# The row-maxima shift of an attention kernel, as four 32-row products for two key tiles at once

## The chip, the cores and the metric

The kernel runs on one core of one Trainium2 chip. The metric is the device time of one execution in microseconds (us); the kernel before takes 3069.19 us, the median of three runs (3068.3 to 3076.0). TensorE (PE) multiplies, VectorE (DVE), ScalarE (ACT) and GpSimd (POOL) work beside it, each with its own queue of instructions in order; they meet through semaphores only.

## The reference

Two layers on `x` of shape (2, 256, 64, 64), all in float32:

```
xn  = group_norm(x, 32 groups)
qkv = qkv_weight @ xn + qkv_bias            # 4 heads of 64 channels, 4096 positions
a   = softmax over the second position of (q^T k) / 8
out = a applied to v, then proj_weight @ out + proj_bias
x1  = x + out
h   = conv3x3(relu(batch_norm(x1)), mean|w0| * sign(w0))
y   = conv3x3(relu(batch_norm(h)),  mean|w1| * sign(w1)) + x1
```

Softmax is exact up to a common factor in a row, so any number can be taken from a row's scores before the exponential. The kernel takes the row's maximum.

## The kernel before, in words

Attention is done for one batch entry and one pair of heads at a time: four **pairs**, one after the other. The two heads of a pair lie on the partitions 0 to 63 and 64 to 127 (`own[0]`, `own[1]`), since a head has 64 channels. Each pair first projects q, k and v (`project`), and splits q and k in two halves of 16 bits each (`q_hi + q_lo`, `k_hi + k_lo`).

Then come 8 **query blocks** of 512 queries (`query_block`, L691), so 32 in all, numbered by `it`. A block walks over 32 **key tiles** (`kt`) of 128 keys in 16 **groups** of two. The scores of one key tile are a 128 x 512 matrix for each head, and fill two PSUM banks; `ps_s` has two slots of two banks, one for the even and one for the odd tile of a group. For each tile (`scores`, L676) TensorE issues three pairs of products (L683: `k_hi q_hi`, `k_lo q_hi`, `k_hi q_lo`), each pair one product for each head, with 64 rows of the array each, side by side. A fourth pair (L688) takes the row maxima off: the left factor `shift` is a matrix with the constant 32768 in the first four rows of each head's half and zero elsewhere, and the right factor `m_rows` has in its first four rows the negated maxima of the 512 queries divided by 32768, each query's in one of the four rows. With the 60 zero rows that is a product of 64 rows too.

ScalarE waits for the tile's count on `s_ready` and takes the exponential of both heads in one instruction of 128 x 1024 (L544) into `prob`, which has six buffers. TensorE multiplies the probabilities by v two tiles later (`values`, L672, float32, both heads side by side as 128 rows by 64 columns). The sums of the probabilities are made by GpSimd (L492; all tiles, or one head alone for 16 of the 32), with the other head of these 16 done by VectorE (L841, L844). GpSimd adds VectorE's half at the end of a block (L495), for which it waits until ScalarE has copied it (`copy_half`, L558), and this ScalarE does behind the exponential of `kt == 1` of the next block. TensorE then adds over partitions (`column_sums`, L663), in group 2 of the next block, or, for the last block of a pair, right behind it.

The maxima of the *next* block are found beside this one: TensorE makes the scores roughly from `k_hi` and `q_hi` alone (`next_maxima`, L648, 64-row pairs into the two banks of `ps_max`), VectorE reduces them (L788), and only then may the next go into the same banks (`mx_used`). A block has 32 of these units: two in a group ("early" and "late"), three in groups 6 and 11 (one more in the middle, "mid"), none in group 15 (`units_of`, L72). The last block of a pair has no next one, and so none. In groups 4 and 5 VectorE also divides the output of the block before (L811, L820). In group 14 it finishes the maxima (L792, L795), in group 15 TensorE turns them into rows (`max_rows`, L655), and VectorE writes `m_rows` from them (`write_max_rows`, L797 to L804, an instruction for each head). TensorE waits for these (`m_rows_done`, L686) ahead of the shift of the block's first tile. For a pair's first block, all this is done before the block starts.

The order of TensorE's work in a group is written out by hand: scores of the even tile, mid, scores of the odd tile, early, (row products in group 15), values of the two tiles before, (column sums in group 2), late. After the two pairs of a batch entry come the output projection and the residual sum, and after all of attention the two convolutions, whose products (L1111) run in 16 steps of 96. The change leaves these alone.

Of the kernel before, what the change touches and what calls it, by code (L numbers as in the profile page):

```python
# [36 lines left out]
QT = TB // P  # L37
# [9 lines left out]
SHIFT = 32768.0  # L47
# [24 lines left out]
def units_of(group):  # L72

    if group >= ROWS_AT:
        return [], [], []
    first = 2 * group + sum(m < group for m in MID_AT)
    if group in MID_AT:
        return [first], [first + 1], [first + 2]
    return [], [first], [first + 1]
# [91 lines left out]
def prologue(nc, x, qkv_t, proj_t, w0_t, par_d, const_d, g):  # L171
    par, const, ones = g.par, g.const, g.ones
    with ExitStack() as ctx:
        def sem(name):
            return ctx.enter_context(nc.semaphore(name))
# [28 lines left out]
        pool_set = sem("pool_set")  # L204
# [3 lines left out]
        @block.sync  # L208
        def _(sp):
            for i in range(B * CB):  # L210
                sp.dma_start(xf[:, i, :], x[i // CB, i % CB]).then_inc(xf_in[i], 16)

            for s in range(2):
                sp.dma_start(g.xn[:, s], x[0, :, :, s * TB:(s + 1) * TB].rearrange("c p n -> p c n")).then_inc(
                    g.xn_in[s], 16)
            sp.dma_start(g.wst[:].rearrange("p c j o -> p (c j o)"), qkv_t[0]).then_inc(g.w_staged, 16)
            sp.dma_start(g.wf[:], w0_t[0]).then_inc(g.wf_in, 16)
# [17 lines left out]
        @block.gpsimd  # L235
        def _(pool):
            nc.gpsimd.memset(ones[:], 1.0).then_inc(pool_set, 1)
            pool.wait_ge(pool_set, 1)

            nc.gpsimd.memset(g.m_rows[:], 0.0).then_inc(pool_set, 1)  # L240
            nc.gpsimd.memset(g.shift[:], 0.0).then_inc(pool_set, 1)
            pool.wait_ge(pool_set, 3)
            for h in range(2):
                s0 = g.own[h].start
                nc.gpsimd.memset(g.shift[s0:s0 + QT, :], SHIFT).then_inc(pool_set, 1)
            pool.wait_ge(pool_set, 5)
            pool.wait_ge(loc_ready, 1)
            nc.gpsimd.partition_all_reduce(g.bound[:], loc[:], P, RMAX).then_inc(bound_ready, 1)

# [95 lines left out]
def attention(nc, x, qkv_t, w0_t, x1_d, g):  # L345
    xt, y32, wst, x1t = g.xt, g.y32, g.wst, g.y_tile
    own, xn, shift, m_rows = g.own, g.xn, g.shift, g.m_rows
    ident = g.const[:, IDENT:IDENT + P]
    mask = g.const[0:QT, MASK:MASK + TB].rearrange("p (a n) -> p a n", a=QT)
    with ExitStack() as ctx:  # L350
        def sem(name):
            return ctx.enter_context(nc.semaphore(name))
# [25 lines left out]
        s_ready = sem("s_ready")  # L378
# [12 lines left out]
        m_rows_done = sem("m_rows_done")  # L391
# [6 lines left out]
        def cols(i, n=TB):  # L398
            return bass.ds(i * n, n)
# [194 lines left out]
        def _(pe):  # L594
            mm = nc.tensor.matmul
# [46 lines left out]
            def next_maxima(it, qb, units):  # L642

                for u in units:
                    t, kb = u // NB, u % NB
                    pe.wait_ge(mx_used, 1 + it * UNITS + u)
                    for h in range(2):
                        last = mm(g.ps_max[:, h], q_hi[own[h], qb * TB + t * P:qb * TB + (t + 1) * P],  # L648
                                  k_hi[own[h], kb * TB:(kb + 1) * TB], start=True, stop=True)
                    last.then_inc(mx_ready, 1)  # L650

            def max_rows(it):
                pe.wait_ge(m_neg_ready, it + 1)
                for h in range(2):
                    last = mm(g.ps_max[0:QT, 1, h * P:(h + 1) * P], m_neg[:, h * QT:(h + 1) * QT], ident,  # L655
                              start=True, stop=True)
                last.then_inc(m_rows_ready, 1)

            def column_sums(it):

                pe.wait_ge(tot_ready, it + 1)
                for h in range(2):
                    last = mm(g.ps_misc[own[h], :], g.ones[:, 0:HD], acc_pool[:, it % 2, h * TB:(h + 1) * TB],  # L663
                              start=True, stop=True)
                last.then_inc(sum_ready, 1)

            def values(n):

                pe.wait_ge(exp_done, n + 1)
                kt = n % KT  # L670
                for h in range(2):
                    last = mm(g.ps_o[own[h], :], vals[:, kt, own[h]], prob[:, n % PBUF, h * TB:(h + 1) * TB],  # L672
                              start=(kt == 0), stop=(kt == KT - 1))
                last.then_inc(g.pv_done, 1)

            def scores(it, qb, kt, first):  # L676

                if kt >= 2 or not first:
                    pe.wait_ge(exp_done, it * KT + (kt - 1))
                keys = slice(kt * P, (kt + 1) * P)  # L680
                for k, q in ((k_hi, q_hi), (k_lo, q_hi), (k_hi, q_lo)):
                    for h in range(2):
                        mm(g.ps_s[:, kt % 2, h], k[own[h], keys], q[own[h], cols(qb)], start=(k is k_hi and q is q_hi),  # L683
                           stop=False)
                if kt == 0:
                    pe.wait_ge(m_rows_done, (it + 1) * 2)  # L686
                for h in range(2):
                    last = mm(g.ps_s[:, kt % 2, h], shift[own[h]], m_rows[own[h], qb % 2], start=False, stop=True)  # L688
                last.then_inc(s_ready, 1)

            def query_block(it, qb):  # L691

                first, last = qb == 0, qb == NB - 1
                for group in range(GROUPS_A):
                    kt = 2 * group
                    mid, early, late = ([], [], []) if last else units_of(group)
                    scores(it, qb, kt, first)
                    next_maxima(it + 1, qb + 1, mid)
                    scores(it, qb, kt + 1, first)
                    next_maxima(it + 1, qb + 1, early)  # L700
                    if group == ROWS_AT and not last:
                        max_rows(it + 1)
                    if group == 1 and not first:
                        pe.wait_ge(o_copied, it + 1)
                    if group or not first:
                        for old in (kt - 2, kt - 1):
                            values(it * KT + old)
                    if group == SUMS_AT and not first:
                        column_sums(it - 1)
                    next_maxima(it + 1, qb + 1, late)  # L710
                if last:
                    for old in (KT - 2, KT - 1):
                        values(it * KT + old)
# [12 lines left out]
            for b in range(0, B):  # L726
                for hp in range(0, 2):
                    pair = b * 2 + hp
                    it0 = pair * NB
                    for s in range(2):  # L730
                        project(b, hp, 0, s, False)
                    for n2 in range(1, NB // 2):
                        for s in range(2):
                            project(b, hp, n2, s, True)
                    for s in range(2):
                        first_maxima(it0, NB // 2 - 1, s, range(QT))

                    pe.wait_ge(klo_done, 2 + it0 + NB)
                    pe.wait_ge(qlo_done, 2 + it0 + NB)
                    pe.wait_ge(v_copied, 2 + it0 + NB)  # L740
                    max_rows(it0)
                    for qb in range(NB):
                        query_block(it0 + qb, qb)
                    column_sums(it0 + (NB - 1))

                for n2 in range(0, NB // 2 - 1):
                    for s in range(2):
                        output_projection(b, n2, s, 1)
                output_projection(b, NB // 2 - 1, 0, 1)
                output_projection(b, NB // 2 - 1, 1, 0)  # L750

        @block.vector
        def _(dve):
# [43 lines left out]
            def write_max_rows(it, slot):  # L797

                dve.wait_ge(m_rows_ready, it + 1)
                for h in range(2):  # L800
                    s0 = own[h].start
                    v.tensor_tensor(m_rows[s0:s0 + QT, slot].rearrange("p (a n) -> p a n", a=QT),  # L802
                                    g.ps_max[0:QT, 1, h * P:(h + 1) * P].unsqueeze(1).to_broadcast([QT, QT, P]),
                                    mask, ALU.mult).then_inc(m_rows_done, 1)  # L804
# [473 lines left out]
```

## Time and profile before

| | us |
|---|---|
| median of three runs | 3069.19 |
| profiled execution, its own time | 3075.72 |
| its span, from the first to the last instruction | 3073.9 |
| mean granted TensorE clock | 0.972 of 2.4 GHz |

```
engine                       busy us   share of span
PE (matmul)                   2829.9   92%
DVE                           2145.2   70%
POOL                          2025.5   66%
ACT                           1390.7   45%
```

TensorE is busy in 92% of the span, but products overlap in the records, so that this is no measure of its load: the start times of products tell it. A product of 512 columns is recorded with 0.38 us, and the next pair starts about 0.22 us after it. The two products of a pair start within 0.01 us of each other, and the views merge them ("x2"). Attention's blocks run from 118 us to about 2650 us of the span, with projections between the pairs. A release that names L688 is the shift, with which a score tile becomes ready for ScalarE.

### The profile page before, as it was taken

The page shows a single profiled execution, that of the slowest core. Times are in us where ns is not written, and L with a number is a line of the kernel's source. Part 1 is how long each engine was busy: PE and PEld are TensorE (multiplying, and loading weights), DVE is VectorE, ACT ScalarE, POOL GpSimd, SP SyncE. Part 2 cuts the span into 40 slices and gives each one's busy share as a digit, 9 for nine tenths or more (in the row PEclk, how much of TensorE's full clock was granted, in tenths as well). Part 3 has the DMA queues.
Part 4 walks back from the last instruction along what each step waited for, and adds up shares of the span by engine and source line. Part 5 has one row for each costly group of instructions (what it writes and reads, how often), then busy time and mean ns, then how long its engine had stood idle before and what let it go on. Part 6 is the DMA issues. An engine that isn't in the chain of part 4 may idle for free. (4 is left out here: it accounts for less than half of the span.)

```text
span 3073.9 us, 43595 instructions
## 1 busy us (share of the span) xinstructions
PE 2829.9 (92%) x17060; PEld 1013.5 (33%) x17060; DVE 2145.2 (70%) x2528; ACT 1390.7 (45%) x1461; POOL 2025.5 (66%) x1208
## 2 busy tenths in 40 slices
PE   5799999997999999987999999987999999979898
PEld 3233333323333333333333333342333333334343
DVE  5677777736777777546777777456777776488785
ACT  3354444452545444532544454543454445344342
POOL 2588778783888888843888888855878888520022
PEclk9899999998999999998999999998999999989999
DMA  5000000001000000041000000010000000232032
GB/s 203 33 1 1 1 1 1 1 1 60 1 1 1 1 1 1 1 132 54 1 1 1 1 1 1 1 42 1 1 1 1 1 1 1 71 116 88 0 109 82
DMA packets 26819, 78.27 MB, mean 25 GB/s; under 512 B 1920, under 2 KB 2176, under 8 KB 25600
## 3 DMA queue, kind: packets, MB, share of 16 engines
q1 hardware_dynamic: 25792, 74.19, 6.9%
q8 instruction: 125, 2.05, 0.3%
q10 hardware_dynamic: 832, 1.45, 0.1%
q14 instruction: 70, 0.57, 0.1%
HBM read 58.86 MB, written 16.78 MB: 25 GB/s over the span
## 5 line engine op out<-in xcount | busy, mean ns | idle before, releaser
L492 POOL TENSOR_TENSOR acc_pool<-acc_pool,prob 128x512 f32<-128x512 f32 (+1 forms) x992 | 1779.6, 1794 | 376.9 <-ACT prob L544 269.9
L544 ACT ACTIVATE prob<-ps,exp_scale 128x1024 f32<-128x1024 f32 x1024 | 1091.9, 1111 | 1191.0 <-PE ps L688 1188.5
L788 DVE TENSOR_REDUCE m_part<-ps 128x2 f32<-128x1024 f32 x896 | 1095.2, 1222 | 477.6 <-PE ps L648 453.6
L672 PE MATMUL ps<-prob,vals 128*64 128x512 f32 x4096 | 999.8, 609 | 0.0
L648 PE MATMUL ps<-k_hi,q_hi 64*128 64x512 f16 x1792 | 347.5, 384 | 79.8 <-DVE m_part L788 79.8
L672 PEld LDWEIGHTS ps<-prob,vals 128*64 128x64 f32 x4096 | 250.3, 137 | 498.5 <-issue 367.4
L844 DVE TENSOR_TENSOR ps<-ps,prob 128x512 f32<-128x512 f32 x480 | 331.5, 691 | 91.2 <-ACT prob L544 91.2
L683 PE MATMUL ps<-q_hi,k_hi 64*128 64x512 f16 x2048 | 391.8, 379 | 0.0
L683 PE MATMUL ps<-q_hi,k_lo 64*128 64x512 f16 x2048 | 391.0, 378 | 0.0
L683 PE MATMUL ps<-q_lo,k_hi 64*128 64x512 f16 x2048 | 390.8, 378 | 0.0
L688 PE MATMUL ps<-m_rows,shift 64*128 64x512 f16 x2048 | 390.4, 378 | 0.4
L648 PEld LDWEIGHTS ps<-k_hi,q_hi 64*128 64x128 f16 x1792 | 86.6, 93 | 522.6 <-DVE m_part L788 451.3
L773 DVE TENSOR_REDUCE m_part<-ps 128x2 f32<-128x1024 f32 x128 | 156.9, 1226 | 104.7 <-PE ps L638 104.7
L1111 PE MATMUL ps<-parts,signs 128*128 128x512 f16 x768 | 181.3, 385 | 21.9 <-DVE parts L1170 19.9
L811 DVE RECIPROCAL ps<-ps 128x128 f32<-128x128 f32 x128 | 122.7, 959 | 99.3 <-PE ps L663 99.3
L1111 PE MATMUL ps<-parts,wmid 128*128 128x512 f16 x768 | 179.0, 383 | 0.0
L683 PEld LDWEIGHTS ps<-q_hi,k_hi 64*128 64x128 f16 x2048 | 100.4, 95 | 126.9 <-ACT prob L544 45.5
L688 PEld LDWEIGHTS ps<-m_rows,shift 64*128 64x128 f16 x2048 | 100.0, 94 | 125.8 <-DVE m_rows L802 4.0
L683 PEld LDWEIGHTS ps<-q_lo,k_hi 64*128 64x128 f16 x2048 | 100.2, 95 | 122.9 <-issue 2.7
L609 PE MATMUL ps<-xn,wst 128*128 128x512 f32 x256 | 129.7, 636 | 8.1 <-ACT xn L582 5.2
L683 PEld LDWEIGHTS ps<-q_hi,k_lo 64*128 64x128 f16 x2048 | 100.1, 94 | 111.3 <-issue 1.6
L525 ACT ACTIVATE y<-ps,pair_bias,fscale 128x512 f32<-128x512 f32 x64 | 49.7, 777 | 175.2 <-PE ps L609 127.1
(115 smaller groups left out, 1587.8 us busy)
## 6 DMA issues: line engine op xcount, KB each, us to landing
xt<-in_x SPq DMA_DIRECT2D x40, 512.0 KB, 4.0
xf<-in_x SPq DMA_DIRECT2D x4, 2048.0 KB, 17.0
x_scratch<-y_tile SPq DMA_DIRECT2D x16, 512.0 KB, 5.0
wf<-in_w_t SPq DMA_DIRECT2D x4, 1152.0 KB, 9.9
rows<-x_scratch SPq DMA_DIRECT2D x8, 576.0 KB, 5.1
rows<-x_scratch SPq DMA_DIRECT2D x8, 544.0 KB, 4.6
xn<-in_x SPq DMA_DIRECT2D x8, 512.0 KB, 5.7
xt<-x_scratch SPq DMA_DIRECT2D x4, 1024.0 KB, 5.1
```

Source lines behind the costliest of these rows:

```text
L492: nc.gpsimd.tensor_tensor(acc[:, part], acc[:, part], tile[:, part], ALU.add).then_inc(pool_add, 1)
L544: nc.scalar.activation(prob[:, n % PBUF], g.ps_s[:, kt % 2].rearrange("p h n -> p (h n)"), ACT.Exp, scale=g.exp_scale[:]).then_inc(exp_don ...
L609: ins = mm(g.ps_s[:, s, j], wst[:, c, j, :], xn[:, s, c, :], start=(c == 0), stop=(c == CB - 1))
L648: last = mm(g.ps_max[:, h], q_hi[own[h], qb * TB + t * P:qb * TB + (t + 1) * P], k_hi[own[h], kb * TB:(kb + 1) * TB], start=True, stop=True)
L672: last = mm(g.ps_o[own[h], :], vals[:, kt, own[h]], prob[:, n % PBUF, h * TB:(h + 1) * TB], start=(kt == 0), stop=(kt == KT - 1))
L683: mm(g.ps_s[:, kt % 2, h], k[own[h], keys], q[own[h], cols(qb)], start=(k is k_hi and q is q_hi), stop=False)
L688: last = mm(g.ps_s[:, kt % 2, h], shift[own[h]], m_rows[own[h], qb % 2], start=False, stop=True)
L773: v.tensor_reduce(m_part[:, :, t * NB + (n2 * 2 + s)], g.ps_max, AX.X, ALU.max).then_inc(mx_used, 1)
L788: v.tensor_reduce(m_part[:, :, u], g.ps_max, AX.X, ALU.max).then_inc(mx_used, 1)
L811: v.reciprocal(g.ps_misc[:, c], g.ps_misc[:, c]).then_inc(rec_ready, 1)
L844: v.tensor_tensor(acc_dve, acc_dve, tile, ALU.add).then_inc(dve_add, 1)
L1111: last = nc.tensor.matmul(g.ps[:, 4 * m + pos, :], weights(l, c, pos, dx)[:, m * P:(m + 1) * P], parts[:, s, c, h, pos, :, dx:dx + W], sta ...
```

## The change

The shift leaves `scores` and becomes a step of its own, `shifts`, once a group, behind the scores of both tiles and ahead of the early maxima. It consists of four products of 32 rows: row quarter r holds the constants and maxima rows for head r % 2, and the product goes to tile r // 2 of the group. So quarters 0 and 1 serve the even tile, 2 and 3 the odd one, in four different PSUM banks. `s_ready` rises by two when the last is done, so that both tiles come free for ScalarE at once. The quarters 1 and 3 need rows of their own: `write_max_rows` has four instructions for two, and the setting of `shift` in the prologue four for two.

```diff
@@ prologue, GpSimd
-            for h in range(2):
-                s0 = g.own[h].start
-                nc.gpsimd.memset(g.shift[s0:s0 + QT, :], SHIFT).then_inc(pool_set, 1)
-            pool.wait_ge(pool_set, 5)
+            for r in range(4):
+                nc.gpsimd.memset(g.shift[32 * r:32 * r + QT, :], SHIFT).then_inc(pool_set, 1)
+            pool.wait_ge(pool_set, 7)
@@ attention, TensorE
+            def shifts(it, qb, kt):
+
                 if kt == 0:
-                    pe.wait_ge(m_rows_done, (it + 1) * 2)
-                for h in range(2):
-                    last = mm(g.ps_s[:, kt % 2, h], shift[own[h]], m_rows[own[h], qb % 2], start=False, stop=True)
-                last.then_inc(s_ready, 1)
+                    pe.wait_ge(m_rows_done, (it + 1) * 4)
+                for r in range(4):
+                    quarter = slice(32 * r, 32 * r + 32)
+                    last = mm(g.ps_s[:, r // 2, r % 2], shift[quarter], m_rows[quarter, qb % 2], start=False, stop=True)
+                last.then_inc(s_ready, 2)
@@ query_block, TensorE
                     scores(it, qb, kt, first)
                     next_maxima(it + 1, qb + 1, mid)
                     scores(it, qb, kt + 1, first)
+                    shifts(it, qb, kt)
                     next_maxima(it + 1, qb + 1, early)
@@ write_max_rows, VectorE
-                for h in range(2):
-                    s0 = own[h].start
+                for r in range(4):
+                    s0, h = 32 * r, r % 2
```

## Rows read from the trace of the kernel before

**Rows 1.** Page: the shift's products (count; busy us, mean ns; idle before).
```profile
L688 PE MATMUL ps<-m_rows,shift 64*128 64x512 f16 x2048 | 390.4, 378 | 0.4
```
**Rows 2.** Timeline of PE, an ordinary group (start us, us, what, count).
```profile
1000.05 0.38 PE L683 MATMUL ps<-q_hi,k_hi 64*128 64x512 f16 x2
...
1001.56 0.38 PE L688 MATMUL ps<-m_rows,shift 64*128 64x512 f16 x2
1001.77 0.38 PE L648 MATMUL ps<-k_hi,q_hi 64*128 64x512 f16 x2
1002.08 1.94 PE L672 MATMUL ps<-prob,vals 128*64 128x512 f32 x8
1003.95 0.39 PE L648 MATMUL ps<-k_hi,q_hi 64*128 64x512 f16 x2
1004.18 0.38 PE L683 MATMUL ps<-q_hi,k_hi 64*128 64x512 f16 x2
```
**Rows 3.** Stretch of group 7: us, busy of PE, PEld, DVE, ACT, POOL.
```profile
1012.80:1016.90 4.10, 4.10 (x30) 1.38 (x28) 3.63 (x5) 2.12 (x2) 3.08 (x3) 1.00 0.00 0
```
**Rows 4.** Timeline of PE, groups 6 and 11: maxima that wait for VectorE.
```profile
1006.68 0.38 PE L688 MATMUL ps<-m_rows,shift 64*128 64x512 f16 x2
1008.33 0.59 PE L648 MATMUL ps<-k_hi,q_hi 64*128 64x512 f16 x2 [1.27 <-DVE m_part L788]
...
1030.41 0.39 PE L648 MATMUL ps<-k_hi,q_hi 64*128 64x512 f16 x2 [0.46 <-DVE m_part L788]
...
1032.13 0.39 PE L648 MATMUL ps<-k_hi,q_hi 64*128 64x512 f16 x2 [0.47 <-DVE m_part L788]
```
**Rows 5.** A pair's last block: waits, GpSimd's groups 622.8 to 685.3, timeline.
```profile
PE ps L663 <- POOL acc_pool L495: 22.8, 4, 5.7
...
L492 POOL TENSOR_TENSOR acc_pool<-acc_pool,prob 128x512 f32<-128x512 f32 (+1 forms) x31 | 55.6, 1794 | 4.4
...
621.62 1.27 POOL L495 TENSOR_TENSOR acc_pool<-acc_pool,half_sum 128x512 f32<-128x512 f32 x1 [1.04 <-ACT half_sum L558]
...
618.88 2.12 ACT L544 ACTIVATE prob<-ps,exp_scale 128x1024 f32<-128x1024 f32 x2 [2.23 <-PE ps L688]
```
**Rows 6.** Changes of tile shape: weight loads (group 5), group 15, line L655.
```profile
1002.56 0.14 PEld L672 LDWEIGHTS ps<-prob,vals 128*64 128x64 f32 x2 [0.29 <-ACT prob L544]
1002.99 0.14 PEld L672 LDWEIGHTS ps<-prob,vals 128*64 128x64 f32 x2 [0.28 <-issue]
...
1048.45 0.38 PE L688 MATMUL ps<-m_rows,shift 64*128 64x512 f16 x2
1048.89 0.60 PE L655 MATMUL ps<-const,m_neg 128*4 128x128 f32 x4
1049.42 1.94 PE L672 MATMUL ps<-prob,vals 128*64 128x512 f32 x8
...
L655 PE MATMUL ps<-const,m_neg x128: 272/273/421, 115.9 to 2590.8; 128*4 128x128 f32 x128
```
**Rows 7.** Timelines of DVE and PE: rows of maxima written, next block's scores.
```profile
1049.53 1.39 DVE L802 TENSOR_TENSOR m_rows<-ps,const 4x512 f16<-4x512 f32 x2
...
1051.29 0.39 PE L683 MATMUL ps<-q_hi,k_hi 64*128 64x512 f16 x2
```
**Rows 8.** Timeline at the start of a pair's first block.
```profile
765.36 1.39 DVE L802 TENSOR_TENSOR m_rows<-ps,const 4x512 f16<-4x512 f32 x2 [1.20 <-PE ps L655]
...
768.91 0.64 PE L648 MATMUL ps<-k_hi,q_hi 64*128 64x512 f16 x2
...
770.87 0.39 PE L648 MATMUL ps<-k_hi,q_hi 64*128 64x512 f16 x2 [1.32 <-DVE m_part L788]
```
**Rows 9.** Stretches at half clock (as rows 3, then PEclk); values in one.
```profile
359.60:363.00 3.40, 3.15 (x8) 0.87 (x10) 2.02 (x3) 0.14 (x1) 3.11 (x3) 0.54 0.00 0
...
2407.60:2411.00 3.40, 3.31 (x10) 0.86 (x10) 1.86 (x3) 0.00 (x0) 3.11 (x3) 0.54 0.01 2
...
1008.85 3.38 PE L672 MATMUL ps<-prob,vals 128*64 128x512 f32 x8
```

## The prediction

> **What bounds the kernel now.** I read the page first for what the change touches: 2048 shift products of 0.38 us each, with no idle time ahead of them, so TensorE comes to them with everything ready [rows 1]. Next the order in time on TensorE for one ordinary group. The reader is to look at start times, not at durations. From 1000.05 to 1001.77 eight pairs start, one every 0.215 us: that is a pair's price, and of the recorded 0.38 us the rest lies under the next pair. Two of the eight are shifts. Then come the values and the late maxima, and the same point of the next group is at 1004.18: 4.13 us a group, without a gap [rows 2]. In such a group TensorE sets the pace: the other engines are busy for less than its 4.10 us, VectorE 3.63, GpSimd 3.08, ScalarE 2.12 [rows 3].
>
> Not every group is like that. Where three maxima stand in a group, TensorE waits for VectorE: in group 6 for 1.27 us, since VectorE comes late out of the divisions of groups 4 and 5, and in group 11 twice for some 0.47, because a maximum can't follow the last sooner than 1.72 us (1030.41 to 1032.13), the time of product, reduction and release [rows 4]. In group 15 the products on the maxima's rows start 0.44 us after the last shift, where 0.31 is what a change of work costs elsewhere [rows 2, 6]: that is a wait for VectorE too. So of 16 groups five (4, 5, 6, 11 and 15) have VectorE's pace, and 11 have TensorE's. There are 4 x 7 = 28 blocks that look ahead, so 28 x 11 = 308 groups in which a change of TensorE's work counts in full. The last block of a pair is another case: GpSimd adds 31 tiles there with 4.4 us of idle time in all, and TensorE then waits for it at the column sums, four times, 22.8 us in sum [rows 5]. That block ends with GpSimd, and faster products there buy nothing.
>
> **The shift's products.** Removed are two pairs, 2 x 0.215 = 0.43 us a group. Added are four products of 32 rows. If they run side by side as pairs do now, they take one slot of 0.215, and about 0.01 for two more starts. On this alone the group would be 0.205 us shorter. But now a third shape of tile stands in the middle of the 64-row products, and what it costs to change the shape can be read. From the last 64-row pair to the values (128 rows, 64 columns) it is 0.31 us, where a pair takes 0.215: 0.095 more [rows 2]. The other way, the values' four pairs at 0.43 each [rows 6] make 1.72, and the next 64-row pair starts 1.87 after the first of them [rows 2]: 0.15 more, of which 0.095 would be the way out and 0.055 the slower loading at the way in. For the 16-bit pair that follows, the way in costs 0.01 (0.39 us for 0.38, [rows 2]). A third case has 128 rows on both sides and differs in columns alone: four products on the maxima's rows at (0.60 - 0.27) / 3 = 0.11 make 0.44, and the values start after 0.53: 0.09 more [rows 6]. So every change of shape in this trace costs 0.09 on the way out and 0.01 to 0.055 on the way in. None shows 32 rows beside 64. I take for it what all the others have, with the way in of 16-bit data, 0.10 for one change and 0.20 for two. New price: 0.215 + 0.01 + 0.20 = 0.425, for 0.43 before. Over 308 groups that is -1.5 us, and as the rows have only hundredths, **0 +- 3 us**. The bounds: with no change to pay, -0.205 a group, -63 us; with two at 0.15, 0.525 for 0.43, +29 us.
>
> The Trainium skill (TensorEngine Tiling (Array Packing), Key Properties) says that going to another tiling mode, not just to another tile, drains TensorE. The 0.09 us above [rows 2, 6] is what such a drain costs here, and the page would have it for 32 rows against 64 as well; by it the sum is the 0 just taken. The same skill (TensorE: Matmul & The Clock Gate, Part 3, measured speedup) has four row tiles of 32 with 512 columns at 3.07 times the speed of one after another. An estimate from it is 0.86 / 3.07 = 0.28 us for the four and not 0.225, +0.055 a group, +17 us; no run here shows that yet.
>
> **The even tile comes later.** Its shift used to start behind its own scores; now it waits for the odd tile's scores, some 0.65 + 0.10 us. Both exponentials follow at once, 2.12 us in all, from 0.42 us after the shift started [rows 5], counted from the shift of the same group, so they end 1.5 and 2.6 us after the new shift. Who waits for them? The next even scores start 0.31 + 0.31 + 1.87 + 0.23 = 2.7 us after the shift (maxima, values, maxima), the next odd ones at 3.4, and values a whole group later: cover of 1.2 and 0.8 us. In the last blocks, without maxima, these are 0.31 + 1.87 = 2.2 and 2.8 us against 1.5 and 2.6: still cover, 0.2 at the least. **0 us**; were it gone there, GpSimd still ends last. VectorE adds a tile's half only behind a maximum that starts later. 0.
>
> There is one place without cover. At a pair's last block GpSimd is the bound, and before it starts its 32 tiles it waits 1.04 us for ScalarE's copy of the half sum, which stands behind the second exponential of the block [rows 5]. Now: exponentials from 618.88, done at 621.00. After: the scores of both tiles are six pairs, which end where the old second shift's start less 0.215 was, so the new shift starts about 0.12 us before the old second one did, 0.74 after the old first one, and the exponentials and the copy are 0.75 us later. GpSimd's chain moves with them: 4 x 0.75 = **+3 us**. For the 28 other blocks this copy is late too, but the column sums wait for it only in group 2, over 4 us later: 0.
>
> **The rows of maxima.** VectorE writes four times, not twice; two took 1.39 us, so four take 2.8, and from 1049.53 they end at 1052.33. TensorE needs them ahead of the new shift: the next block's scores start at 1051.29, six pairs make 1.30 and the change of shape 0.09, so 1052.68 [rows 7]. Cover 0.3 us, thin; each 0.1 us that is lacking would cost 28 x 0.1 = 3 us. VectorE itself has no maxima in group 15. At a pair's first block the writing is open to view: from 765.36 four end at 768.16, so a shift at 768.2, and at the half clock of that stretch early maxima 0.43 + 0.2 later, 768.85, for 768.91 now; what comes next waits at 770.87 for the reduction of just these [rows 8]. **0**. Two more settings in the prologue are small work of an engine that has nothing else to do there. 0.
>
> **The clock.** In group 6 TensorE's idle time is sometimes followed by 3.4 us at half clock (0.54 as the mean of the stretch, so 1.2 GHz); there are six such stretches, one in the group 6 of six of the 28 blocks. The values then take 3.38 us for 1.94 and the maxima ahead 0.59 for 0.39: 1.6 us each [rows 2, 4, 9]. In groups 5 and 6 the wait on VectorE stays and TensorE has less to stream around it, so I count one more, **+2 us**.
>
> **Sum.** 0 + 3 + 0 + 2 = +5 us. The profiled execution took 3075.72 (its span 3073.9 and 1.8 around it), 6.5 above the median of 3069.19, and would take 3080.7; the median becomes **3074 us**.
>
> **Rivals.**
> A. *32 and 64 rows change without a drain*, both being cuts of the same rows. Then 308 x 0.205 = 63 us go: 3074 - 63 = **3011**. The other engines would allow it: early maxima come 1.95 us behind late ones now and may come 1.72 behind, so 0.23 is to be had there [rows 2, 4]. Against it: each of the kinds of change that the trace has costs the same, even where the rows stay 128.
> B. *The four don't run side by side*, but two and two, for a port or a bank that four share. Then the change saves nothing and pays the two changes of shape: +0.215 x 308 = 66, **3140**. It decides from the point where the third product starts a slot behind the first. For it: nothing in the trace has more than two tiles at once. Against: the two products of a pair start within 0.01 us and write two banks; here four write four. This is the rival on the other side.
> C. *The clock falls in every group 6*: 22 more times 1.6 is 35, less the 2 counted, **3107**. For it: the idle time is in each block. Against: it takes it in six of 28 now, and the change adds no wait there.
> D. *A change of shape is dearer than 0.10*, with four weights to load at once, 0.15 as before the values: +29, **3103**.
>
> **How the numbers follow.** My forecast 0.53, with a range of its own from 3066 to 3083 (the +-3, one to three stretches of clock, cover that fails a little); A 0.18; D 0.11; C 0.07; B 0.07; 0.04 for others. From no change a measurement of this kernel can tell about 0.3%, 9 us. Within it: most of the forecast, 0.52. Faster: A and a rest, 0.20. Slower: D, C, B and a rest, 0.28. The range goes from A to C, 3006 to 3110; left out are B, the lower edge of A and others, some 0.15.
>
> **What would show it.** In the order in time on TensorE: the four shift products start within 0.02 us; the first of them 0.31 after the last scores, the early maxima 0.31 to 0.33 after it; an ordinary group still 4.13 us from point to point. If the distances are 0.215, A is right, and the group is 3.9; if third and fourth start 0.2 later, B. The exponentials come in twos right behind each other, and GpSimd's add of the half in a pair's last block is 0.75 us later against the block's first scores. Six to eight stretches at half clock in group 6. The forecast is wrong if an ordinary group differs from 4.13 by more than 0.03 us.

## The result and the profile after

The changed kernel takes 3083.0 us (13 runs, 3072.5 to 3089.0) for 3068.7 (13 runs of the kernel before beside them): 1.0045 times the time, interval 1.0032 to 1.0058. A later batch gave 3082.1 (5 runs) and a ratio of 1.0037 (1.0023 to 1.0051). The prediction was 3074 with a range of 3006 to 3110. So the time lies in the range and near the forecast, but 9 us above it, and beyond the 0.3% that I had called no change. One execution of the kernel before, in the batch of the first experiments, took 4911.8 us at a granted clock of 0.607 and is left out of every median and mean. The profiled execution took 3082.3 us, with a span of 3080.5 and a mean granted clock of 0.969.

The page has the shift's products at half their busy time (203 us for 390), as four of 32 rows now stand side by side:

```profile
L691 PE MATMUL ps<-m_rows,shift 32*128 32x512 f16 x2048 | 203.2, 387 | 1.3 <-DVE m_rows L806 1.3
```

The time did not follow. The timeline of TensorE for an ordinary group, as [rows 2] has it for before (start us, us, what, count):

```profile
1044.76 0.39 PE L647 MATMUL ps<-k_hi,q_hi 64*128 64x512 f16 x2
1044.98 0.38 PE L682 MATMUL ps<-q_hi,k_hi 64*128 64x512 f16 x2
...
1046.06 0.38 PE L682 MATMUL ps<-q_lo,k_hi 64*128 64x512 f16 x2
1046.37 0.40 PE L691 MATMUL ps<-m_rows,shift 32*128 32x512 f16 x4
1046.70 0.39 PE L647 MATMUL ps<-k_hi,q_hi 64*128 64x512 f16 x2
1047.02 1.94 PE L671 MATMUL ps<-prob,vals 128*64 128x512 f32 x8
1048.89 0.39 PE L647 MATMUL ps<-k_hi,q_hi 64*128 64x512 f16 x2
1049.12 0.38 PE L682 MATMUL ps<-q_hi,k_hi 64*128 64x512 f16 x2
```

The reader is to see three distances. From the last scores to the shift it is 0.31 us, from the shift to the maxima 0.33, where pairs of one shape follow each other in 0.215: two changes of tile shape at 0.1 each, one on each side of the shift. And the record of the four lasts 0.40 us for 0.38, so they do run side by side. The group is 4.14 us from 1044.98 to 1049.12, for 4.13 before. The slot that was saved has been paid out again.

At a pair's last block, GpSimd and ScalarE, for [rows 5]:

```profile
621.68 2.12 ACT L543 ACTIVATE prob<-ps,exp_scale 128x1024 f32<-128x1024 f32 x2 [2.24 <-PE ps L691]
...
624.43 1.27 POOL L494 TENSOR_TENSOR acc_pool<-acc_pool,half_sum 128x512 f32<-128x512 f32 x1 [1.05 <-ACT half_sum L557]
...
688.17 1.97 PE L662 MATMUL ps<-acc_pool,ones 128*64 128x512 f32 x4 [7.43 <-POOL acc_pool L494]
```

The block's first scores start at 619.83, so the exponentials are 1.85 us behind them (before 618.88 - 617.80 = 1.08). From the add of the half sum to the column sums nothing has moved: 63.74 us for 63.71. TensorE now waits there for 7.43 us, 5.7 before: it is ready about 0.9 us earlier, and GpSimd comes 0.8 later, both against the block's first scores.

The four writes of maxima rows, for [rows 7]; the second row is the shift behind them:

```profile
618.07 2.82 DVE L806 TENSOR_TENSOR m_rows<-ps,const 4x512 f16<-4x512 f32 x4
...
621.23 0.40 PE L691 MATMUL ps<-m_rows,shift 32*128 32x512 f16 x4
```

They end at 620.89; the shift starts 0.31 us after the last scores (620.92), as everywhere, so it did not wait.

Last, group 6 and the clock, for [rows 4, 9]. In the stretches the third figure from the end is the granted clock; there are seven like these in the 28 blocks that look ahead, the first and the last shown.

```profile
1008.11 0.39 PE L647 MATMUL ps<-k_hi,q_hi 64*128 64x512 f16 x2 [0.82 <-DVE m_part L792]
...
1009.08 0.39 PE L691 MATMUL ps<-m_rows,shift 32*128 32x512 f16 x4
1010.62 0.61 PE L647 MATMUL ps<-k_hi,q_hi 64*128 64x512 f16 x2 [1.16 <-DVE m_part L792]
1011.16 3.23 PE L671 MATMUL ps<-prob,vals 128*64 128x512 f32 x8
...
361.60:365.00 3.40, 3.19 (x10) 0.86 (x10) 1.97 (x3) 1.22 (x2) 3.26 (x2) 0.54 0.00 0
...
2413.00:2416.40 3.40, 3.11 (x8) 0.87 (x10) 2.06 (x3) 1.31 (x2) 3.26 (x2) 0.54 0.00 0
```

A block without such a stretch takes 71.1 us from first exponential to first exponential in both kernels, and one with it 72.7 to 72.8.

### The profile page after: what moved, and what is told of

The parts are those of the page before. It is cut to its first block and busy times, and to the rows that moved or that the text cites. A ratio compares the mean times of both kernels' runs of the same rounds, so it can differ in the third digit from the quotient of the medians.

```text
span 3080.5 us, 43661 instructions
## 1 busy us (share of the span) xinstructions
PE 2821.7 (92%) x17060; PEld 966.5 (31%) x17060; DVE 2188.8 (71%) x2592; ACT 1381.8 (45%) x1461; POOL 2025.5 (66%) x1210
## 5 line engine op out<-in xcount | busy, mean ns | idle before, releaser
L691 PE MATMUL ps<-m_rows,shift 32*128 32x512 f16 x2048 | 203.2, 387 | 1.3 <-DVE m_rows L806 1.3
L1065 ACT ACTIVATE parts<-comb 128x512 f16<-128x512 f32 x128 | 77.4, 632 | 105.8 <-DVE comb L1195 105.8
```

The costliest lines, as they stand in the source:

```text
L691: last = mm(g.ps_s[:, r // 2, r % 2], shift[quarter], m_rows[quarter, qb % 2], start=False, stop=True)
```

## The experiments

Each run comes with its granted clock, and since the clock is either full or half, twice (1 - clock) times the span is its time at half clock. The table has, beside the median time, the means over the runs of each kernel. The last column takes off half of the time at half clock, as if TensorE had set the pace throughout it (a pair of products then takes 0.43 us for 0.215). That is the most that can be lost. Among the runs of one kernel the span grows by only about a third of it (a straight line through the runs has a slope of 0.37 for before, 0.33 for changed).

| kernel | runs | median us | clock | at half clock, us | span less half of it |
|---|---|---|---|---|---|
| before | 20 | 3070.1 | 0.9741 | 159 | 2988 |
| changed | 13 | 3083.0 | 0.9690 | 191 | 2985 |
| before, again | 11 | 3071.7 | 0.9736 | 162 | 2989 |
| changed, again | 5 | 3082.1 | 0.9702 | 184 | 2987 |
| order alone | 11 | 3064.8 | 0.9765 | 144 | 2992 |
| order, one pair | 4 | 2996.2 | 0.9718 | 169 | 2911 |
| before, divisions moved | 5 | 3052.1 | 0.9764 | 144 | 2979 |
| changed, divisions moved | 5 | 3056.9 | 0.9752 | 152 | 2979 |
| 32 rows at each tile | 4 | 3234.8 | 0.9765 | 152 | 3155 |
| behind the maxima | 5 | 3120.0 | 0.9734 | 166 | 3035 |
| order alone, copy ahead | 6 | 3062.2 | 0.9767 | 143 | 2989 |
| changed, copy ahead | 12 | 3073.8 | 0.9713 | 176 | 2984 |
| the fastest | 5 | 3044.8 | 0.9754 | 150 | 2969 |

**Before and changed, again.** The same kernels; only clocks and stretches are wanted.

> The kernel before, run as an experiment of its own, so that each of its runs comes with its granted clock. The changed kernel's 13 runs have mean clocks from 0.966 to 0.972, and their times lie between 3089 and 3073 in the same order: half of the time at half clock is lost. Theory 1 (the surplus of the change over my sum, some 9 us, is time at half clock): runs of before lie at a higher clock than those of after, 0.970 to 0.975, and time less (1 - clock) x span is the same for both kernels within 3 us. Theory 2 (the surplus is a wait in every run, in the first blocks and at the ends of the pairs): the clocks are alike, about 0.969, and that corrected time is 10 us or more lower for before. Time against before: the same within 0.2% in both.

> The changed kernel once more, beside the same runs of before as the next three. In the first batch before had a mean granted clock of 0.974 in 31 runs, and the order alone (64-row products behind both tiles' scores) 0.9765 and 3065 us. Time less (1 - clock) x span: changed 2985, before 2988, order alone 2992. If the whole surplus of the change is time at half clock: again 3081 to 3084, clock 0.969, in its profile six to nine stretches of 3.4 us behind the wait of group 6, where the order alone had none in 28 blocks and before four to six.

Before against before has a ratio of 1.0005 (0.9996 to 1.0014). Its clock is 0.0046 above that of the changed kernel, and less half of the time at half clock the two are 3 us apart, the changed one lower; with a third in place of the half the changed one is some 2 us higher. Theory 1 holds either way: the surplus is mostly time at half clock. Its profile has four stretches at half clock in group 6 (289.1, 504.1, 1756.8 and 2401.9), that of [rows 9] six. The changed kernel has six in its second profile, seven in its first.

**The order alone**, against the kernel before:

```diff
-                for h in range(2):
-                    last = mm(g.ps_s[:, kt % 2, h], shift[own[h]], m_rows[own[h], qb % 2], start=False, stop=True)
-                last.then_inc(s_ready, 1)
+            def shifts(it, qb, kt):
...
+                for t in range(2):
+                    for h in range(2):
+                        last = mm(g.ps_s[:, t, h], shift[own[h]], m_rows[own[h], qb % 2], start=False, stop=True)
+                last.then_inc(s_ready, 2)
@@ query_block
                     scores(it, qb, kt + 1, first)
+                    shifts(it, qb, kt)
```

> Only the order of the change: the four shift products keep 64 rows (two pairs), but stand behind the scores of both tiles, and both tiles are released at once. Two writes of maxima rows, no third shape of tile. If the change's price for shape just cancels the slot that it saves (my sum), the ordinary group is 4.13 us here as in both kernels, and GpSimd's chain in a pair's last block is late by 0.85 us (the even tile waits for 0.86 us of products), 3 to 4 us in all: 3069 + 4 = 3073. If the surplus of the change comes with the order (exponentials in twos, more time at half clock around group 6), this kernel has it too: 3080 to 3085. If it comes with 32-row products (less load on TensorE, so a lower clock, or the four writes of rows), this one stays at 3073.

3064.8 us, 0.9985 of before (0.9976 to 0.9994): faster, which none of my cases had. The group is what it was:

```profile
1007.20 0.38 PE L683 MATMUL ps<-q_hi,k_hi 64*128 64x512 f16 x2
...
1008.28 0.38 PE L683 MATMUL ps<-q_lo,k_hi 64*128 64x512 f16 x2
1008.49 0.59 PE L691 MATMUL ps<-m_rows,shift 64*128 64x512 f16 x4
1008.93 0.38 PE L648 MATMUL ps<-k_hi,q_hi 64*128 64x512 f16 x2
1009.24 1.94 PE L672 MATMUL ps<-prob,vals 128*64 128x512 f32 x8
...
1011.33 0.38 PE L683 MATMUL ps<-q_hi,k_hi 64*128 64x512 f16 x2
```

4.13 us, with 0.21 ahead of the shift and 0.44 (two slots) for it. And in 28 blocks there is no stretch at half clock in group 6, though TensorE waits there nearly as long as in the changed kernel (0.82 and 1.05 us, for 0.82 and 1.16):

```profile
1002.26 0.39 PE L648 MATMUL ps<-k_hi,q_hi 64*128 64x512 f16 x2 [0.82 <-DVE m_part L792]
...
1003.14 0.59 PE L691 MATMUL ps<-m_rows,shift 64*128 64x512 f16 x4
1004.78 0.39 PE L648 MATMUL ps<-k_hi,q_hi 64*128 64x512 f16 x2 [1.05 <-DVE m_part L792]
1005.10 1.94 PE L672 MATMUL ps<-prob,vals 128*64 128x512 f32 x8
...
1001.40:1004.80 3.40, 1.53 (x16) 0.53 (x14) 3.29 (x5) 1.03 (x2) 3.11 (x3) 1.00 0.00 0
```

So the surplus comes with the 32-row products (or the four writes, which this kernel doesn't have either), not with the order. The order alone has the late exponentials as well: in its last blocks the column sums start 68.46 us behind the first scores, for 67.54 before and 68.34 in the changed kernel.

**32 rows at each tile**, the price of a change of shape by itself, in the kernel before:

```diff
-                    last = mm(g.ps_s[:, kt % 2, h], shift[own[h]], m_rows[own[h], qb % 2], start=False, stop=True)
+                    rows = slice(own[h].start, own[h].start + 32)
+                    last = mm(g.ps_s[:, kt % 2, h], shift[rows], m_rows[rows, qb % 2], start=False, stop=True)
```

> The kernel before with one thing changed: the two shift products of a tile have 32 rows (0 to 31 and 64 to 95) in place of 64, where they stood. No slot is saved, and each tile pays two changes of shape, so two groups of them a group. By my price of 0.10 for one change, an ordinary group is 4.13 + 0.40 = 4.53 us, and 308 groups make +123 us; group 11 and group 6 absorb theirs: 3069 + 120 = 3190 (3175 to 3205). If 32 rows beside 64 cost nothing (rival A), 3069. If a change costs 0.05, 3130.

3234.8 us, 1.0537 times before (1.0520 to 1.0553).

```profile
1052.12 0.38 PE L683 MATMUL ps<-q_hi,k_hi 64*128 64x512 f16 x2
...
1052.55 0.38 PE L683 MATMUL ps<-q_lo,k_hi 64*128 64x512 f16 x2
1052.87 0.39 PE L689 MATMUL ps<-m_rows,shift 32*128 32x512 f16 x2
1053.18 0.39 PE L683 MATMUL ps<-q_hi,k_hi 64*128 64x512 f16 x2
```

0.32 and 0.31 us where 0.215 stood: rival A is out, and one change costs 0.10 each way. The group is 4.55 us. The total is 45 us above what I expected: a block takes 76.6 us for 71.1, so 28 x 5.5 = 154 and not 123. That is 13 groups' worth of 0.42, where I had counted 11: groups 4 and 5 count in full too (4.55 us each, as the others), and group 6, where VectorE's lateness covers the products, becomes only 0.14 us shorter by it (6.43 for 6.57). The rest lies mainly in the pairs' last blocks (69.7 us for 67.5 from the first scores to the column sums). The clock did not fall here, with 32-row products and twice as many changes of shape: 0.9765, and one stretch at half clock in group 6. So it isn't 32 rows as such that lower it.

**Behind the maxima.** One change of shape fewer, from 32 rows straight to the values:

```diff
                     scores(it, qb, kt + 1, first)
-                    shifts(it, qb, kt)
+                    if group == 0:
+                        pe.wait_ge(m_rows_done, (it + 1) * 4)
                     next_maxima(it + 1, qb + 1, early)
+                    shifts(it, qb, kt)
```

> The changed kernel with the shifts behind the early maxima in place of ahead of them (the wait for the rows of maxima stays ahead of the maxima of group 0). TensorE then goes 64 rows, 32 rows, 128 rows for the values: one change of shape fewer in a group. By my price the ordinary group is 4.03 us, 308 x 0.10 = 31 us less than the changed kernel: 3083 - 31 = 3052, 0.5% below the kernel before. Rival: VectorE or the exponentials, which come 0.3 us later still, take up the 0.10, and the group stays at 4.13: 3083.

3120.0 us, 1.0161 times before (1.0147 to 1.0175): 37 us more than the changed kernel, where the rival said as much as it.

```profile
1025.09 0.39 PE L647 MATMUL ps<-k_hi,q_hi 64*128 64x512 f16 x2
...
1026.40 0.38 PE L682 MATMUL ps<-q_lo,k_hi 64*128 64x512 f16 x2
1026.81 0.39 PE L647 MATMUL ps<-k_hi,q_hi 64*128 64x512 f16 x2
1027.13 0.39 PE L689 MATMUL ps<-m_rows,shift 32*128 32x512 f16 x4
1027.45 1.94 PE L671 MATMUL ps<-prob,vals 128*64 128x512 f32 x8
1029.32 0.39 PE L647 MATMUL ps<-k_hi,q_hi 64*128 64x512 f16 x2
```

The changes are saved as planned, and the early maxima still wait: from the late ones there are only six pairs, 1.52 us, and they can follow in 1.72 at the least [rows 4]. So 1.72 + 0.32 + 0.32 + 1.87 = 4.23 us a group. The shift had stood between two maxima and covered VectorE's time. I had the 1.72 in the prediction and did not apply it here.

**One pair.** The order alone with the odd tile's shift left out:

```diff
-                           stop=False)
+                           stop=kt % 2 == 1 and q is q_lo)
...
-                for t in range(2):
-                    for h in range(2):
-                        last = mm(g.ps_s[:, t, h], shift[own[h]], m_rows[own[h], qb % 2], start=False, stop=True)
+                for h in range(2):
+                    last = mm(g.ps_s[:, 0, h], shift[own[h]], m_rows[own[h], qb % 2], start=False, stop=True)
```

> The order alone (64-row products once a group), with the odd tile's shift left out, so that its exponentials are of scores that nothing was taken from: TensorE's work a group is one pair of 64 rows for the shift and no third shape of tile. This is what the change would be if its two changes of shape cost nothing: an ordinary group 4.13 - 0.215 = 3.91 us. Maxima then follow each other in 1.73 us where 1.72 is the least, so VectorE just allows it. 11 groups of 28 blocks: 3065 - 66 = 2999 (2995 to 3010). If VectorE or GpSimd holds the group above 3.91, the change had no more than that to gain even with free changes of shape.

2996.2 us, 0.9761 of before (0.9747 to 0.9775), and 69 less than the order alone.

```profile
965.60 0.38 PE L683 MATMUL ps<-q_lo,k_hi 64*128 64x512 f16 x2
965.82 0.38 PE L690 MATMUL ps<-m_rows,shift 64*128 64x512 f16 x2
966.03 0.38 PE L648 MATMUL ps<-k_hi,q_hi 64*128 64x512 f16 x2
...
969.95 0.38 PE L648 MATMUL ps<-k_hi,q_hi 64*128 64x512 f16 x2
```

3.92 us from maxima to maxima: no other engine holds the group. So a slot saved would have been worth all of its 0.215, and the two changes of shape took just this. It also bears on the clock: two stretches at half clock came back in group 6, and 169 us in all for the 144 of the order alone, with 64-row products throughout and two writes. The two stretches are 7 of the 25 us. Some 14 stand at the pairs' ends, where TensorE waits for GpSimd ahead of the column sums: 8.2 us here, and the half clock that sets in during the wait lasts 10.2 us in all four pairs; in the order alone the wait is 6.6 and the half clock 6.8. The same 10 us around a wait, this kernel first (the granted clock is again the third figure from the end):

```profile
661.20:671.20 10.00, 5.59 (x9) 1.92 (x10) 3.39 (x6) 0.19 (x1) 4.13 (x3) 0.50 0.00 1
...
680.90:691.10 10.20, 8.68 (x28) 4.30 (x29) 4.75 (x8) 2.81 (x4) 2.54 (x3) 0.68 0.00 1
```

What this kernel shares with the changed one is that TensorE streams one slot less than in the order alone. It is also ready sooner wherever another engine sets the pace: in group 6 it waits 1.03 and 1.27 us, for 0.82 and 1.05 in the order alone, so that less work and a longer wait come together here.

**The divisions moved**, in the kernel before and in the changed one:

```diff
-DIVIDE_AT = {(4, 0): 0, (4, 1): 1, (5, 0): 2, (5, 1): 3}
+DIVIDE_AT = {(3, 0): 0, (4, 0): 1, (4, 1): 2, (5, 0): 3}
```

> The kernel before with VectorE's four divisions at (3,0), (4,0), (4,1), (5,0) in place of (4,0), (4,1), (5,0), (5,1), so that VectorE is not late at the three maxima of group 6. Group 6 should then look like group 11, 5.62 for 6.57 us: 28 x 0.95 = 27 us less, and no stretch at half clock in group 6 (4 to 6 now, 1.6 us each, 8 us): 3069 - 27 - 8 = 3034. If TensorE's wait in group 6 has another source than the divisions: 3069.

> The changed kernel with the same move of the divisions. Theory 1 (the surplus is half clock behind group 6's wait, plus 3 us at GpSimd's chain): without that wait this kernel is only 3 to 6 us above the kernel before with the same move, 3038 to 3040. Theory 2 (a surplus in every block or at the pairs' borders, with no tie to group 6): it stays 12 to 14 us above it, 3047. If 32-row products lower the clock anywhere TensorE waits, group 11 now shows stretches at half clock.

3052.1 us (0.9939, 0.9925 to 0.9952) and 3056.9 us (0.9949, 0.9936 to 0.9963). Of the 27 us that I expected for the shorter wait there were 11: a block is 70.7 us for 71.1 and group 6 still 6.15 where I had 5.62, since VectorE is still late at the first of the three maxima. But neither kernel has a stretch at half clock in group 6 any more, nor one in group 11, and the distance between the two fell from 11 to 14 us to 4.8. Theory 1 said 3 to 6. So 6 to 9 us of the surplus, more than half, seem tied to group 6; the runs of the two reach from 3051.4 to 3055.3 and from 3051.7 to 3059.9, so that this is good to some 4 us only.

**The copy ahead.** In a pair's last block, on the order alone and on the changed kernel:

```diff
+                if last:
+                    copy_half(it - 1)
                 for kt in range(KT):
...
                     if kt == 1 and not first:
-                        copy_half(it - 1)
+                        if not last:
+                            copy_half(it - 1)
                         copy_output(it - 1)
```

> The order alone (64-row products once a group), and in a pair's last block ScalarE copies VectorE's half sum ahead of the block's first exponential in place of behind the second. GpSimd's chain there then starts as soon as its last tile of the block before is added: about 1.0 us earlier than in the order alone, four times, 4 us: 3065 - 4 = 3061. If something else ends these blocks (the column sums or the first exponential), 3065. Theory on the change: of its surplus 3 us come from this copy, which this run measures by itself.

> The changed kernel with the half sum copied ahead of the first exponential in a pair's last block. If the late copy costs the change what I said, GpSimd's chain starts 1.0 us earlier at four places: 3082 - 4 = 3078, with 1.0 us less from the block's first exponential to the column sums (66.49 in the changed kernel). The four writes of rows delay the half sum itself, so it may be 0.5 us and 3080.

3062.2 us (0.9970, 0.9958 to 0.9982), 2.6 less than the order alone; and 3073.8 us for the changed kernel (1.0010, 0.9999 to 1.0020), some 8 less. GpSimd, with the copy ahead of the changed kernel's exponentials:

```profile
616.35 4.87 POOL L491 TENSOR_TENSOR acc_pool<-acc_pool,prob 128x1024 f32<-128x1024 f32 x2 [1.45 <-ACT prob L545]
621.30 1.27 POOL L494 TENSOR_TENSOR acc_pool<-acc_pool,half_sum 128x512 f32<-128x512 f32 x1
```

There is no wait for ScalarE left. From the block's first exponential to the column sums it is 65.29 us for 66.49. But that exponential itself now comes 0.34 us later behind the block's first scores, as the copy stands ahead of it; from these scores to the column sums it is 67.47 us for 68.34, so 0.87 are gained, 3.5 in four pairs. Of the 8 us that the medians show this leaves 4.7; having 8 us less at half clock (176 for 184) would give some 3 of them, and the rest I can't assign.

**The fastest.** Order alone, copy ahead, divisions at (3,0), (3,1), (4,0), (4,1):

> What the runs point to as the fastest: 64-row products once a group, the early copy, and the divisions at (3,0), (3,1), (4,0), (4,1), two half groups ahead of before. With the divisions at (3,0) to (5,0) a block was 70.7 us for 71.1, and group 5 still 5.73 where an undisturbed one is 5.20; without that 0.53 a block is 70.2: 28 x 0.9 = 25 us less than order and copy (3062), 3037, and no stretch at half clock in group 6. If the divisions only move the delay to groups 3 and 4, where there are two maxima and no third, TensorE waits there instead, and it is 3050.

3044.8 us, 0.9922 of before (0.9909 to 0.9935), the fastest complete kernel here; with 70.4 us a block, about halfway between my two cases. It has 64-row products only.

## Why the prediction was right, and where it was not

*Shift products: 0 +- 3 us.* Right, with its working. Four side by side cost one slot and two changes of shape cost 0.10 each (0.31 and 0.33 us around the shift); the group is 4.14 us for 4.13, a block 71.1 for 71.1. The two bounds were tested: without changes of shape 69 us are to be had (I had 63), and with two more pairs of changes a group grows by 0.42. That a change costs the same between 32 and 64 rows was the guess on which all depended, and the chance of 0.18 for rival A was fair for a shape that the trace did not have. The drain of the Trainium skill (TensorEngine Tiling (Array Packing), Key Properties) is thus shown here with its price. The estimate from its other page (the Trainium skill, TensorE: Matmul & The Clock Gate, Part 3, measured speedup) of 0.28 us for the four is not borne out: the group would be 4.18 us, and of the 0.33 from the shift to the maxima 0.10 are the change of shape, which leaves 0.23.

*How many groups count: 308.* Too few, since groups 4 and 5 have TensorE's pace and not VectorE's. The block without a slot is 68.5 us for 71.1, 12 groups' worth (13 groups are shorter by a slot, and group 6 is longer by one, 6.78 us for 6.57), and the one with dearer groups 13's. As the price of a group was next to nothing, this did no harm to the sum.

*The even tile later: 0, and +3 at the last blocks.* Right in its reading, too much for the total. No scores and no values wait for an exponential in an ordinary group; in the last blocks scores wait for one eight times, 1.8 us in all, at no cost, as GpSimd ends last. GpSimd's chain is 0.8 us late against the first scores in each of four blocks, 3.2 us.

*The rows of maxima: 0.* Right in the other blocks (no wait at 621.23, cover 0.3). In a pair's first block it is 73.8 us for 73.4 from `m_neg` (the negated maxima, made ahead of the block) to the second block's first exponential. That isn't a term beside the last one. An exponential stands 0.77 us further behind its scores in every block, so by its scores the second block comes 0.3 us earlier. Over a whole pair, from `m_neg` to the column sums of the last block, both are in: with the divisions moved, where no block has a stretch at half clock, it is 564.4 and 564.6 us in two pairs of the changed kernel and 563.9 to 564.1 in the four of before. (The other two pairs of the changed kernel take 566.0 and 567.5, with 9.6 and 14.6 us at half clock for about 8.) So all that is late comes to 0.5 us a pair, **2 us** in all; 3.2 and four times 0.45 would count the later exponential twice.

*The clock: +2 us.* This term failed by its size, and it is what puts the result outside 0.3%. I counted stretches in the one profile I had, six, and added one. The changed kernel's profiles have seven and six, so that this looks right; but the count in before's execution was high for it: again it had four, and its mean clock over 20 runs is 0.974, for 0.969. In time at half clock the kernels differ by 191 - 159 = 32 us, and by 22 in the later batch. With the third that the runs of one kernel lose of it, an estimate, that is 11 and 7 us. With the wait of group 6 shortened, 6 to 9 us of the surplus go. The profiles show less than that in group 6 itself: seven and six for six and four, at 1.65 us each (72.77 us for a block of 71.12). Rival C had the mechanism, in a size (every block) that did not come. The sign was right, and "less to stream around it" fits: the order alone (a slot more, no stretch), one pair (a slot less, two stretches, 64 rows) and the changed kernel (a slot less and two changes of shape, six and seven) go up in this row. What is not shown is that the load alone decides. One pair's waits in group 6 are the longest of the three, with fewer stretches than the changed kernel, so the length of the wait alone doesn't either. Two executions of one kernel have stretches in different blocks and in different number, and in these kernels the blocks also lie at other times; no run holds one fixed and moves the other.

What I had not thought of at all are the pairs' ends. TensorE waits 7.2 to 7.5 us there for GpSimd, 5.7 before, and the half clock around this wait lasts 10.2 us in two of the four pairs in either profile of the changed kernel; in the two profiles of the kernel before it lasts 6.8 in all eight. Ten us around such a wait, changed and before:

```profile
2662.40:2672.60 10.20, 5.75 (x9) 2.08 (x10) 3.56 (x7) 2.20 (x2) 4.17 (x3) 0.50 0.00 0
...
2657.50:2667.70 10.20, 7.26 (x15) 2.84 (x16) 4.79 (x9) 2.14 (x2) 2.81 (x2) 0.69 0.00 1
```

Added up: 2 us of delays, 0 for the groups, and 11 and 7 us for the clock: 13 and 9, for 13 to 14 and 11 measured. With the divisions moved the same sum is 2 + 8/3 = 5 for 4.8. What stays open is how much of the clock's part belongs to group 6, how much to the pairs' ends and how much to their first blocks, where the changed kernel is at half clock for longer in some executions (in its profile one first block took 71.7 us and another 68.9). So the products and the delays were right within 1 us, by mechanism and size; the clock was short by 5 to 9, and the median of 3083.0 stands at the upper edge of the forecast's own range, 3066 to 3083.

## What to carry to other kernels

A row tile that is cut finer saves its slots only if its neighbours have the same shape: count the changes on both sides, 0.1 us each here, against the 0.215 us of a slot, before counting the tiles. When an order is changed, take the least distance between two steps that hand a buffer back and forth, and check it in the new order. And an added or saved slot beside a long wait of TensorE can count twice, as the clock behind the wait went with it here: to size that, many runs' mean clock says more than the stretches of one profile. Last, when a delay is added up from several places, measure it once from end to end, or the same 0.8 us is counted twice.

## What the hardware showed that I had not expected

Where work was taken from TensorE beside its waits, its clock was lower. Waits of about 1 us in group 6 had no half clock behind them in 28 blocks with 64-row shifts once a group (0.82 and 1.05 us), in two blocks with one such pair fewer (1.03 and 1.27 us), and in six or seven with the four of 32 rows (0.82 and 1.16 us). At the pairs' ends, over the profiles of all the kernels here, a wait of 7.9 to 8.2 us went with 10.2 us at half clock in 4 of 4 cases, one of 7.2 to 7.5 with 10.2 in 6 of 20 and 6.8 in the others, one of 5.6 to 6.6 with 6.8 in 24 of 24, and one of 2.8 (32 rows at each tile) with none in 3 of 4. And putting two shifts of 64 rows behind the odd tile, next to that wait, without any work saved, made the kernel 0.15% faster than before, 144 us at half clock for 159.
